# Moving four VectorE additions behind two PSUM evacuations in an eight-core recurrent layer

## The reference, cut to what matters

```python
# x: (16, 2048, 2048) f32; d = 2048
xn = layernorm(x)
# branch s: recurrent block of rank 8 and a small feed-forward of rank 32
xn_ = layernorm(xn) * ln_gamma + ln_beta
u   = xn_ @ W_in + b_in                       # (.., 8)
h   = scan(h[t] = sigmoid(decay_logit) * h[t-1] + u[t])
x2  = xn + h @ W_out + b_out + xn_ * D_skip
hf  = relu((layernorm(x2)*gamma + beta) @ W_down + b_down)   # (.., 32)
s   = x2 + hf @ W_up + b_up
# branch g: 8-bit fake-quantised 2048 x 2048 matmul
y   = relu(fake_quant(xn) @ fake_quant(ffn_kernel) + fake_quant(ffn_bias))
g   = silu(fake_quant(y))                     # scale from the row's maximum of y
out = x + s * g
```

## Time and profile before

| | us |
|---|---|
| median of 3 runs | 2352.27 (2352.03 to 2353.75) |
| the profiled execution's own time | 2355.56 |
| its span, from the first to the last instruction of the slowest core (core 6) | 2354.0 |
| spans of the other cores | 2349.1 to 2353.8 |
| TensorE matmul busy | 1378.3 (59%) |
| VectorE busy | 1153.6 (49%) |
| ScalarE busy | 732.3 (31%) |
| GpSimd busy | 298.7 (13%) |

### The profile page before, as it was taken

How to read it: one execution, slowest core, us unless ns; L and a number is a source line. 1 busy time by engine, 2 the same in 40 slices (tenths; PEclk the granted TensorE clock), 3 DMA queues, 4 the chain that set the end, 5 groups by cost and what they waited for, 6 DMA issues and landing times.

```text
span 2354.0 us, 27052 instructions; the slowest of 8 cores (2349.1 to 2354.0 us)
## 1 busy us (share of the span) xinstructions
PE 1378.3 (59%) x5025; PEld 580.7 (25%) x5025; DVE 1153.6 (49%) x2855; ACT 732.3 (31%) x772; POOL 298.7 (13%) x132
## 2 busy tenths in 40 slices
PE   1343343366666666666666666666666666666664
PEld 0222222222222222222222222222222222222221
DVE  4333333345555555555555555555555555555552
ACT  0211212123333333333333333333333333333332
POOL 0000000001111111111111111111111111111111
PEclk9999999986666666666666666666666666666666
DMA  1111121101111111111111111111111111111110
GB/s 23 46 40 50 36 53 37 54 1 37 36 36 37 36 36 36 37 36 37 36 36 36 36 36 36 36 36 37 36 37 37 36 36 39 42 37 37 36 36 27
DMA packets 56491, 86.47 MB, mean 37 GB/s; under 512 B 11118, under 2 KB 44014, under 8 KB 52206
## 3 DMA queue, kind: packets, MB, share of 16 engines
q1 hardware_dynamic: 56348, 84.75, 14.5%
HBM read 51.17 MB, written 33.55 MB: 36 GB/s over the span
## 4 chain that ended last, share of the span: by engine, by line
DVE 35%; PE 31%; issue 15%; ACT 12%; POOL 3%; DVEq 2%; SPq 1%; ACTq 0%; DMA 0%; POOLq 0%
PE py L701 15%; DVE x L608 4%; DVE x2tmp L607 4%; PE pb L410 3%; PE pb L376 3%; POOL s L788 3%; PE pb L569 3%; DVE t L450 3%; DVE s L678 3%; DVE st L475 3%; ACT xn L469 3%; DVEq L73 2%; DVE t L718 2%; DVE u_sb L577 2%; DVE kstat L385 2%
## 5 line engine op out<-in xcount | busy, mean ns | idle before, releaser
L701 PE MATMUL py<-kq,ixqT 128*128 128x512 bf16 x2048 | 596.1, 463 | 149.9 <-DVE t L721 118.6
L788 POOL TENSOR_TENSOR s<-g,s 128x1024 f32<-128x1024 f32 x64 | 150.1, 2345 | 2034.1 <-ACT g L783 1889.4
L701 PEld LDWEIGHTS py<-kq,ixqT 128*128 128x128 bf16 x2048 | 234.6, 115 | 523.9 <-issue 393.5
L632 ACT ACTIVATE sqscr<-x 128x512 f32<-128x512 f32 x128 | 80.6, 630 | 413.7 <-DVE x L608 411.2
L457 ACT ACTIVATE st<-nw 128x2 f32<-128x2 f32 x32 | 6.6, 206 | 614.4 <-DVE nw L456 614.4
L513 PE MATMUL pb<-eyeb,xnb 128*128 128x128 bf16 x512 | 112.2, 243 | 125.8 <-DVE xnT L517 88.4
L792 POOL TENSOR_TENSOR o<-s,x 128x1024 f32<-128x1024 f32 x64 | 149.7, 2340 | 17.5 <-POOL s L788 17.5
L530 PE MATMUL pb<-eyeb,qbf 128*128 128x128 bf16 x512 | 125.9, 265 | 12.1 <-ACT qbf L485 1.4
L413 DVE CAST kq<-pb 128x512 bf16<-128x512 f32 x64 | 44.3, 692 | 161.0 <-PE pb L410 161.0
L646 DVE CAST r2row<-pff 1x128 bf16<-1x128 f32 x32 | 8.9, 278 | 213.0 <-PE pff L645 213.0
L534 DVE CAST ixqT<-pb 128x512 bf16<-128x512 f32 x128 | 88.6, 692 | 49.9 <-PE pb L530 49.2
(11 more groups left out here) (174 smaller groups left out, 1884.4 us busy)
## 6 DMA issues: line engine op xcount, KB each, us to landing
x<-L_attn_x SPq DMA_DIRECT2D x32, 1024.0 KB, 8.4
out<-o SPq DMA_DIRECT2D x64, 512.0 KB, 3.8
xn<-L_ffn_kernel SPq DMA_DIRECT2D x128, 64.0 KB, 2.2
s<-L_ffn_kernel SPq DMA_DIRECT2D x128, 64.0 KB, 2.2
wint<-L_attn_W_in SPq DMA_DIRECT2D x16, 4.0 KB
wdnt<-L_attn_W_down SPq DMA_DIRECT2D x16, 16.0 KB
x<-L_attn_W_up SPq DMA_DIRECT2D x1, 256.0 KB
eyef<-c_eye_f SPq DMA_DIRECT2D x1, 64.0 KB
```

What stands on the lines that cost most here:

```text
L632: sq.append(S(deps, lambda e, q=q: e.activation(sqscr[:], x2_t[:, 512 * q:512 * (q + 1)], AF.Square, bias=0.0, scale=1.0, accum_out=st[:, ...
L701: mmlast = T(deps, lambda e, j=j, qq=qq, fofs=fofs, ixb=ixb: e.matmul(py[qq][:], ixb[:, 128 * j:128 * (j + 1)], kq[:, D * j + fofs:D * j + ...
L788: sg = G([e4, rc["s1"], rc.get("tap_s")], lambda e, h=h: e.tensor_tensor(sb_[:, 1024 * h:1024 * (h + 1)], g_t[:], sb_[:, 1024 * h:1024 * ( ...
```

## The change

The four additions L678 leave `emit_mid2` and become a function of their own, `emit_slast`, which the main loop calls after `emit_big_evacs(c, 0)`. The matmuls that they read stay where they were. Line numbers after the moved code grow by 4, those of the additions become L683.

```diff
@@ emit_mid2
                 rc[f"wup{q}"] = wu
+            return
+
+        def emit_slast(c):
+            rc = R[c]
             sb_ = s_t[c % 2]
+            wdst = [pb4, pff[0], pff[1], pff[2]]
             dep_s_free = R[c - 2].get("sg1") if c >= 2 else (KCOL1_FREE if c == 1 else None)
             slast = None
             for q in range(NQ):
                 slast = V([rc[f"wup{q}"], dep_s_free, slast], lambda e, q=q: e.tensor_tensor(
                     sb_[:, 512 * q:512 * (q + 1)], x2_t[:, 512 * q:512 * (q + 1)], wdst[q][:], OP.add))
             rc["s1"] = slast
-            return
@@ main loop
                 emit_mid2(c)
                 emit_big_evacs(c, 0)
+                emit_slast(c)
                 emit_big_half(c, 1)
```

More of the change, by code:

```diff
@@ L830, in build_nc @@
                         emit_mid2(c)
+                        if "last" not in R[c]:
+                            emit_slast(c)
                 if TRUNC == 3:
```

## The result

| | before | after |
|---|---|---|
| median of 8 runs, us | 2353.35 | 2307.58 |
| profiled execution, us | 2355.56 | 2308.58 |
| its span, slowest core, us | 2354.0 (core 6) | 2307.0 (core 0) |

The ratio is 0.9813, with a 95% interval of 0.9797 to 0.9830. It is a ratio of means, as are those further down; of the medians it is 0.9806, since one of the eight runs took 2321.71 us with a lower clock on one die. The forecast was 2307 from a median of 2352.3, 45 us less; measured are 45.8 us less.

The account below looks back on a forecast made before the run. It took a chain through VectorE and ScalarE to bound the kernel, no engine being above 59% busy. Saving 25 (next chunk's start) + 3.6 (last chunk) + 16 (half 0's clock) = 45 us from 2352.3 gave 2307, range 2289 to 2327.

Parts of the forecast that it names:

- The path: After hfaug, in 31 chunks: VectorE's start of L450 counts; half 1's earlier start alone is worth nothing there.
- The start of the next chunk: From hfaug's start to L450: 4.84 us instead of 5.65, saving 0.81 a chunk, 25 us over 31.
- The clock in half 0: Half 0's clock rise, no longer always late, shortens it from some 9.74 to 9.21 us: 16 us over 31 chunks.
- a balance that holds the period: Half 0 starting later meets the rise sooner, keeping 58.02 us a chunk; 0.8 us less a chunk loses this.
- only the direct part: Rival: half 0's rise stays late, perhaps with the new period at another balance; 2323.5 us, chance 0.15.
- The last chunk: Nothing follows on VectorE, so half 1 is the path and its earlier start saves 3.6 us once.
- Starts of half 0: Sign in the changed profile: half 0 starts 56.5 to 57 us apart, against 58.02 before.
- Half 1 was to wait: Sign at half 1's start, after hfaug: TensorE waits under 0.3 us instead of 3.66.
- The wait of the transposes: Sign on TensorE before the first transposes L513: idle time grows from 0.40 to over 3 us.
- The rival of the 0.81 level: Rival: denser TensorE work brings grant 0.81 to half 0 in all chunks; 35 us come back, 2342, chance 0.06.
- VectorE was not slowed beside the matmuls: Answers the slower rival: PSUM reads beside matmuls stretch additions from 0.69 to 1.38 us; 2409 us, chance 0.03.

Follow-up runs that it names:

- e1: The changed kernel with the fourth addition done twice, so half 1 stays early but the next chunk's statistics are late again; 2349.41 us.
- e2: The changed kernel with the four additions between the two evacuations, so the statistics are early but half 1 is late; 2305.81 us.
- e3: The kernel before with three tiny dependent VectorE instructions ahead of the next chunk's statistics; 2355.23 us.
- e11: The kernel before with seven tiny dependent VectorE instructions ahead of the next chunk's statistics; 2378.92 us.
- e6: The changed kernel with all four additions moved on into VectorE's wait for xn, except in the last chunk; 2243.82 us.
- e10: The kernel with split additions (three in xn's wait, the fourth behind y's quantisation scalars), plus four small TensorE steps put inside half 0; 2133.81 us.
- e4: The changed kernel with two tiny dependent VectorE instructions ahead of the next chunk's statistics; 2326.61 us.
- e7: The changed kernel with three additions moved into VectorE's wait for xn and the fourth behind the scalars of y's quantisation; 2224.11 us.

## Why the prediction was right, point by point

**The path.** VectorE's queue to L450 and not half 1's start is what counts: shown by e1 and e2, which set them against each other.

**The start of the next chunk.** Forecast 0.81 us a chunk and 25 us; measured 5.66 - 4.84 = 0.82, by 31 is 25.4.

**The clock in half 0.** Forecast 0.53 us a chunk and 16 us; measured is half 0 to `hfaug` 13.49 - 13.01 = 0.48, by 31 is 15. The reason given, a balance that holds the period and is lost with a chunk 0.8 us shorter, is borne out from both sides: e1 brings it back at 58.04 us, e3 shows that it absorbs 0.51 us, e11 that it doesn't absorb 1.6. But e6 and e10 stand in a balance again with still shorter chunks, at 54.61 and 51.19 us, so the rival "only the direct part", a new period in another balance, would have been the right one for some other shorter chunk; the prediction's rows don't show for which. That the mean came out at the middle is in part luck: the distances climb and drop between 2.6 and 6.0 us, and in the kernels without a balance half 0's mean was 9.2 us here and in e2, but 8.9 in e11 and 9.4 in e4 and e7. With means like these the term would have been 9 us larger or 6 smaller.

**The last chunk.** Forecast 3.6, measured 3.0 on the cores compared (50.1 from half 0's start to the end, now 47.2). The three terms are 43.4 us, of the 43.8 between the two cores' spans (2350.8 and 2307.0). The 45.8 us of the medians are 2 more, since this trace of the kernel before is of a core 1 us below the median's slowest, and that of the changed kernel 1 us above.

**What was not as written.** Starts of half 0 were to be 56.5 to 57 us apart; their mean is 56.7, but single ones are 55.6 to 57.7. Half 1 was to wait under 0.3 us; in the chunk shown it waits 0.36. The wait of the transposes was to grow to over 3 us; it is 2.0 in the chunk shown and 2.8 in the mean (85.7 us in 31 waits), since half 1, starting sooner, meets its own rise later; it takes 9.86 us in the chunk shown. It has slack for that. The Trainium skill's rule ("TensorE: Matmul & The Clock Gate", section on oscillation in real kernels) that each burst behind a gap pays for the ramp again cost nothing at the transposes, as the rows said: the first eight took 2.05 us behind the longer gap, and 2.00 before. The rival of the 0.81 level did not come: no core of the profiled run shows it, nor any of the experiments' profiles, while before it stood in the first chunks of die 1 only. The same page of the Trainium skill says in its note on the peak-current limiter that three cores with dense matmuls bring a die to that level; with eight cores and halves of some 9 us, the traces here agree with it on one die of one profile, and for its first chunks alone. VectorE was not slowed beside the matmuls: additions 0.68 to 0.69.

## What to carry to other kernels

When an in-order engine waits for something at the head of its queue, look at what is ready behind it, and ask which of the two chains that leave the place is the path; here the visible 118.6 us of TensorE's wait were worth 3 us, and the 28.2 us of VectorE's wait 25 directly and some 15 more through the clock. Where a loop's period comes out constant, test with a small delay: if it costs nothing, the period is held by something outside the chain, and a change of the path will be worth more or less than its own length. The next wait of the same kind was larger than the first: the same four additions in another place gave 84 us more.

## What was not expected of the hardware

The same kind of delay had three prices: 0.1 us a chunk for 0.51 us in the kernel before, 0.6 for 0.41 in the changed one, and 0.8 for 1.61 in the kernel before again (each the difference of the medians by 31). All follow from half 0 taking half a microsecond more for each microsecond by which the clock's rise is later, 8.41 us at PEclk 0.86 to 9.91 at 0.71 in the rows of e11. And a burst of eight 512-column fillers lifted the clock ahead of its use only to see it fall again: with the pauses filled in part it was back at 0.50 when half 0 began. With 7.07 us for a half at 1.00 throughout (e10), the 9.2 us of half 0 in the changed kernel still hold 2.1 us of slow clock in each chunk.
